# Causal mask of one-head score groups: from a TensorE matmul into VectorE's maximum

## What is computed

```
x = x + attention(layernorm(x))     # 32 query heads, 8 key/value heads, 64 wide, rotary, causal
x = x + ffn(layernorm(x))           # per-token int8 quantisation, one 256 x 256 product
scores = q @ k.T / 8;  scores = where(causal, scores, lowest float)
attn = softmax(scores);  out = attn @ v;  out @ Wo
```

## Time and profile before

| | |
|---|---|
| time, median of 3 runs | 802.25 us (799.59 to 802.53) |
| profiled execution, first to last instruction | 803.9 us |
| PE busy | 761.0 us (95%), 8230 matmuls |
| DVE busy | 629.2 us (78%), 1392 instructions |
| ACT busy | 628.4 us (78%), 1734 instructions |
| POOL busy | 569.1 us (71%) |
| mask matmuls (L720) | 352, of them 256 of one head |

### The profile page before, as it was taken

One profiled execution on the slowest core, in us unless ns is written; L12 is line 12 of the kernel. 1 busy time (PEld: TensorE's weight loads), 2 busy tenths in 40 slices (PEclk: granted clock), 3 DMA queues, 4 the chain that ended last, 5 costly groups with the idle time before them and its releaser, 6 DMA issues.

```text
span 803.9 us, 23412 instructions
## 1 busy us (share of the span) xinstructions
PE 761.0 (95%) x8230; PEld 640.0 (80%) x8230; DVE 629.2 (78%) x1392; ACT 628.4 (78%) x1734; POOL 569.1 (71%) x524
## 2 busy tenths in 40 slices
PE   5799999999999999999999999999999999999993
PEld 3578888888888887788888888888888888888782
DVE  5757787777787887777788888887788877877887
ACT  4577888787877887787788778887788778888873
POOL 3467868787768786877786887778686787686402
PEclk9899999999999999999999999999999999999996
DMA  8255544554555554455554455455454555454300
GB/s 267 56 119 114 130 119 118 132 141 111 127 121 108 118 118 93 117 117 119 115 121 108 113 128 120 104 128 122 106 117 107 122 116 126 93 116 97 87 8 27
DMA packets 56994, 90.99 MB, mean 113 GB/s; under 512 B 12592, under 2 KB 19248, under 8 KB 56880
## 3 DMA queue, kind: packets, MB, share of 16 engines
q1 hardware_dynamic: 53808, 79.02, 43.0%
q0 software_dynamic: 3072, 10.49, 5.0%
HBM read 16.06 MB, written 2.10 MB: 23 GB/s over the span
## 4 chain that ended last, share of the span: by engine, by line
PE 71%; DVE 6%; ACT 6%; SPq 5%; issue 5%; DMA 5%; POOL 2%; ACTq 0%; POOLq 0%; DVEq 0%
PE x_bank L621 21%; PE t_bank L733 14%; PE o_bank L749 11%; PE s_bank L717 9%; PE s_bank L718 8%; DMA qT<-wv 4%; PE s_bank L720 3%; PE t_bank L621 3%; PE ot_bank L800 2%; ACT prob L1028 2%; SPq L303 2%; DVE probT L1356 2%; SPq L337 1%; SPq L341 1%; DVE o_norm L1391 1%
## 5 line engine op out<-in xcount | busy, mean ns | idle before, releaser
L1028 ACT ACTIVATE prob<-s_bank,neg_max 128x384 f32<-128x384 f32 (+3 forms) x512 | 266.1, 530 | 64.9 <-DVE neg_max L1367 64.8
L1367 DVE TENSOR_REDUCE neg_max<-s_bank 128x1 f32<-128x384 f32 (+3 forms) x352 | 215.6, 635 | 60.3 <-PE s_bank L720 57.3
L1356 DVE SCALAR_TENSOR_TENSOR probT<-t_bank,probT 128x512 f16<-128x512 f32 x320 | 215.4, 681 | 29.6 <-ACT probT L1040 28.8
L1040 ACT ACTIVATE probT<-t_bank 128x512 f16<-128x512 f32 x320 | 189.0, 600 | 43.8 <-PE t_bank L733 38.8
L733 PE MATMUL t_bank<-ident,prob 128*128 128x128 f32 x1280 | 199.1, 278 | 5.1 <-DVE probT L1356 1.7
L717 PE MATMUL s_bank<-kT,qT 128*128 128x384 f32 (+3 forms) x512 | 178.3, 363 | 6.7 <-DMA qT<-wv 4.2
L491 POOL TENSOR_TENSOR wv<-raw,wv 128x512 fp32r<-128x512 f32 x62 | 79.4, 1280 | 134.2 <-ACT wv L989 134.2
L718 PE MATMUL s_bank<-kT,qT 128*128 128x384 f32 (+3 forms) x512 | 157.1, 322 | 0.0
L733 PEld LDWEIGHTS t_bank<-ident,prob 128*128 128x128 f32 x1280 | 137.6, 141 | 15.0 <-issue 7.5
L749 PE MATMUL o_bank<-value,probT 128*128 128x64 f16 x3840 | 138.5, 193 | 0.0
L749 PEld LDWEIGHTS o_bank<-value,probT 128*128 128x128 f16 x3840 | 131.4, 98 | 6.1
(11 more groups left out here) (123 smaller groups left out, 946.8 us busy)
## 6 DMA issues: line engine op xcount, KB each, us to landing
qT<-wv SPq DMA_DIRECT2D x248, 128.0 KB, 2.4
swp<-raw SPq DMA_DIRECT2D x320, 64.0 KB, 2.0
kT<-key_pair SPq DMA_DIRECT2D x128, 128.0 KB, 2.4
wg_raw<-in_w_group POOLq DMA_DIRECT2D x16, 384.0 KB, 4.9
wg_raw<-in_w_group POOLq DMA_DIRECT2D x16, 256.0 KB, 4.3
resid<-in_x SPq DMA_DIRECT2D x4, 512.0 KB, 7.5
out<-resid SPq DMA_DIRECT2D x16, 128.0 KB, 2.1
wo_stage<-in_w_out SPq DMA_DIRECT2D x4, 256.0 KB, 3.5
```

What stands on the lines that cost most here:

```text
L1028: nc.scalar.activation(prob[:, slot:slot + blocks, h, :], s_bank[G % SCORE_BANKS][:, at * n:(at + 1) * n].rearrange("p (k n) -> p k n", n= ...
L1040: nc.scalar.activation(turned_half[B % TURNED][HI], t_bank[B % TURN_BANKS][:, :], ACT.Copy, scale=PROB_SCALE).then_inc(probT_hi, 1)
L1356: nc.vector.scalar_tensor_tensor(out=turned_half[B % TURNED][LO], in0=t_bank[B % TURN_BANKS][:, :], scalar=PROB_SCALE, in1=turned_half[B % ...
L1367: nc.vector.tensor_reduce(neg_max[:, s % 2, u:u + len(heads)], s_bank[G % SCORE_BANKS][:, 0:len(heads) * n].rearrange("p (h n) -> p h n", ...
```

## The change

Groups with one head lose their mask matmul; their second score matmul signals instead. Their maximum becomes one tensor_tensor_reduce: it adds a row of 0 and -3e38 (mask_row, 512 columns in bf16, of which the last n are taken) to the bank, multiplies with -1, writes the result back into the bank and gives its minimum as neg_max. Their exponential reads the bank with scale -1. Groups 0, 9 and 10 stay as they are. To make room in SBUF the statistics get 8 slots instead of 16, in_inv shares the memory of root_t, and ones lies in an unused part of prob.

```
-        mask = sb("mask", [P, P], bf16)
+        mask_row = sb("mask_row", [P, SEQ], bf16)
...
-        stats = sb("stats", [P, TOK_TILES, 6], f32)
+        stats = sb("stats", [P, STATS, 6], f32)
...
-        in_inv = sb("in_inv", [P, TOK_TILES], f32)
+        in_inv = root_t
...
+        ones = prob[:, 3, 3, :].bitcast(bf16)[:, 0:P]
...
-            nc.gpsimd.memset(mask[:, :], 0.0).then_inc(const_zeroed, 1)
+            nc.gpsimd.memset(mask_row[:, :], 0.0).then_inc(const_zeroed, 1)
...
-                    nc.tensor.matmul(bank, q, kT[s % 2][:, LO, 0:n], start=False, stop=False, skip_group_check=True)
-                diagonals = s_bank[G % SCORE_BANKS][:, 0:len(heads) * n].rearrange("p (h n) -> p h n", n=n)[:, :, i * P:n]
-                nc.tensor.matmul(diagonals, ident_b[:, :], mask[:, :].unsqueeze(1).broadcast_to([P, len(heads), P]),
-                                 start=False, stop=True, skip_group_check=True).then_inc(scores_done, 1)
+                    last = nc.tensor.matmul(bank, q, kT[s % 2][:, LO, 0:n], start=False, stop=(len(heads) == 1),
+                                            skip_group_check=True)
+                if len(heads) > 1:
+
+                    diagonals = s_bank[G % SCORE_BANKS][:, 0:len(heads) * n].rearrange("p (h n) -> p h n", n=n)[:, :, i * P:n]
+                    last = nc.tensor.matmul(diagonals, ident_b[:, :],
+                                            mask_row[:, SEQ - P:SEQ].unsqueeze(1).broadcast_to([P, len(heads), P]),
+                                            start=False, stop=True, skip_group_check=True)
+                last.then_inc(scores_done, 1)
...
+                                     scale=-1.0 if len(SCORE_GROUPS[a][1]) == 1 else 1.0,
...
-                nc.vector.tensor_reduce(neg_max[:, s % 2, u:u + len(heads)],
-                                        s_bank[G % SCORE_BANKS][:, 0:len(heads) * n].rearrange("p (h n) -> p h n", n=n),
-                                        AX.X, ALU.max, negate=True).then_inc(max_done, 1)
+                if len(heads) > 1:
+                    nc.vector.tensor_reduce(neg_max[:, s % 2, u:u + len(heads)],
+                                            s_bank[G % SCORE_BANKS][:, 0:len(heads) * n].rearrange("p (h n) -> p h n", n=n),
+                                            AX.X, ALU.max, negate=True).then_inc(max_done, 1)
+                else:
+
+                    if G == 1:
+                        dve.wait_ge(const_ready, 6)
+                    bank = s_bank[G % SCORE_BANKS][:, 0:n]
+                    nc.vector.tensor_tensor_reduce(bank, bank, mask_row[:, SEQ - n:SEQ], -1.0, UNBOUNDED, ALU.add, ALU.min,
+                                                   neg_max[:, s % 2, u:u + 1]).then_inc(max_done, 1)
```

More of the change, by code:

```diff
@@ L27 @@
 MASKED = -3.0e38
+UNBOUNDED = 3.4e38
 PROB_SCALE = 2.0 ** 14
@@ L47 @@
 LN_STEPS = 5
+STATS = 2 * Q_TILES
 def attention_ffn_kernel(nc: bass.Bass, x: bass.AP, w_group: bass.AP, w_value: bass.AP, w_out: bass.AP,
@@ L76, in attention_ffn_kernel @@
         ident_b = sb("ident_b", [P, P], bf16)
-        mask = sb("mask", [P, P], bf16)
+        mask_row = sb("mask_row", [P, SEQ], bf16)
         zero = sb("zero", [P, 1], f32)
         magic = sb("magic", [P, 2], f32)
-        ones = sb("ones", [P, P], bf16)
         pow_rows = sb("pow_rows", [P, KV_HEADS], f32)
@@ L397, in _ @@
             load_group_weights(0)
-            nc.gpsimd.memset(ones[:, :], 1.0).then_inc(const_ready, 1)
+            nc.gpsimd.memset(ones, 1.0).then_inc(const_ready, 1)
             nc.gpsimd.memset(ident[:, :], 0.0).then_inc(const_zeroed, 1)
             nc.gpsimd.memset(ident_b[:, :], 0.0).then_inc(const_zeroed, 1)
-            nc.gpsimd.memset(mask[:, :], 0.0).then_inc(const_zeroed, 1)
+            nc.gpsimd.memset(mask_row[:, :], 0.0).then_inc(const_zeroed, 1)
             nc.gpsimd.memset(zero[:, :], 0.0).then_inc(const_zeroed, 1)
@@ L408, in _ @@
                                         pattern=[[-1, P]], channel_multiplier=1).then_inc(const_ready, 1)
-            nc.gpsimd.affine_select(out=mask[:, :], in_=mask[:, :], compare_op=ALU.is_ge, fill=MASKED, base=0,
+            nc.gpsimd.affine_select(out=mask_row[:, SEQ - P:SEQ], in_=mask_row[:, SEQ - P:SEQ], compare_op=ALU.is_ge, fill=MASKED, base=0,
                                     pattern=[[-1, P]], channel_multiplier=1).then_inc(const_ready, 1)
@@ L677, in _ @@
             for k in range(K_TILES):
-                last = nc.tensor.matmul(o_bank[:, :], ones[:, :], wv_abs[k], start=(k == 0), stop=(k == K_TILES - 1))
+                last = nc.tensor.matmul(o_bank[:, :], ones, wv_abs[k], start=(k == 0), stop=(k == K_TILES - 1))
             last.then_inc(wv_summed, 1)
@@ L1207, in done_statistics @@
                 dve.wait_ge(resid_added, part_no(s, f % Q_TILES) + 1)
-                nc.vector.bn_stats(stats[:, f, :], resid[:, t, :]).then_inc(stats_done, 1)
+                nc.vector.bn_stats(stats[:, f % STATS, :], resid[:, t, :]).then_inc(stats_done, 1)
             def tile_statistics(t):
-                nc.vector.bn_stats(stats[:, t, :], resid[:, t, :]).then_inc(stats_done, 1)
+                nc.vector.bn_stats(stats[:, t % STATS, :], resid[:, t, :]).then_inc(stats_done, 1)
             def aggregate(first_tile, end_tile, done):
@@ L1216, in aggregate @@
                     dve.wait_ge(stats_done, done + end_tile)
-                    nc.vector.bn_aggr(mean_var[:, t, :], stats[:, t, :]).then_inc(aggr_done, 1)
+                    nc.vector.bn_aggr(mean_var[:, t, :], stats[:, t % STATS, :]).then_inc(aggr_done, 1)
                 dve.wait_ge(aggr_done, done + end_tile)
```

## The result

The changed kernel takes 792.75 us (median of 4 runs, 791.54 to 793.81); the kernel before took 802.39 us beside it (4 runs, 799.59 to 803.44). The ratio is 0.9856 with a 95% interval of 0.983 to 0.9881, so 9.5 to 13.6 us are saved. The profiled execution took 792.76 us, with a span of 791.0 us.

A forecast was written before the change was run, and what follows sets the result against it. Up to turn 1, TensorE was taken to pace even steps and ScalarE's queue of exponentials odd ones. 16 x 0.45 + 16 x 0.15 = 9.6 us off the 802.25 us median gave 793 us, range 779 to 816.

The forecast's parts named there:

- The sum: Whole loop: 0.45 us saved in each of 16 even steps and 0.15 in each of 16 odd, 9.6 us.
- The mask's price: TensorE: a mask costs 0.07 us before transposes, 0.12 before score or projection matmuls; 25 us over the run.
- the rival that gives TensorE nearly everything: Whole loop: TensorE gets back nearly all 25 us of masks, 777 us (half way 785); chance 0.10.
- e: VectorE, each one-head maximum: time the accumulated minimum adds to the pass, taken as 0.09 us.
- rival on a dear e: VectorE's maxima: e from 0.125 to 0.165 us cancels the gain, chance 0.20; dearer makes it slower, chance 0.27.
- 5.5 e: Each step's path: e is paid about 5.5 times, for maxima 1 to 5 and 6 in part.
- The break-even at 0.145: VectorE's maxima: the forecast gain, 0.3 us a step on average, is used up at e of 0.145 us.
- the slower rivals: Maxima 1 to 5 set the pace from e of 0.165 us; 810 us at 0.19, 820 at 0.25; chance 0.27.
- The odd step: ScalarE's exponentials pace up to turn 1; TensorE keeps 0.15 us, from ScalarE's 0.1 and masks 7 and 8.
- The low half of block 0 starts when it did: VectorE, odd step, after maxima 1 to 5: closing gaps of 0.39 us offset 5 x 0.09 = 0.45 us.
- The queries' waits: TensorE, group 0: waits for the queries' DMA, 4.2 us over the run, move with the query path and stay.
- Even steps: TensorE keeps about 0.45 us; exponentials of groups 5 and 6 some 0.4 earlier, groups 7 and 8 about 0.25.

The follow-up runs named there:

- e11: The kernel before, unchanged, profiled a second time: 804.05 us in one run.
- e12: The changed kernel, unchanged, profiled a second time: 795.93 us in one run.
- e5: The changed kernel with a one-column ScalarE copy added in every step between block 0's copy and group 3's exponential: 794.41 us, ratio 0.988.
- e1: The changed kernel with the mask of one-head groups left out altogether, using the old tensor_reduce and old exponential: 791.17 us, ratio 0.9835.
- e3: The changed kernel with two one-element VectorE memsets ahead of each one-head maximum: 795.5 us, ratio 0.9887.
- e9: The changed kernel with the second pair of query placements put ahead of the half swap on SyncE: 794.15 us, ratio 0.9872.
- e10: The kernel before with the second pair of query placements put ahead of the half swap on SyncE: 801.76 us, ratio 0.9952.

## Why the prediction was right, point by point

**The sum.** 0.45 us in an even and 0.15 us in an odd step were predicted. Over all four kinds of step it is 0.51 and 0.43 in even, 0.21 and 0.11 in odd steps, 0.47 and 0.16 in the mean: 16 times both is 10.1 us, where the prediction had 9.6 (10.4 if the kinds are weighted by their steps, ten without and six with a quantised tile on either side). Steps 17 and 18 came at 21.83 and 22.13 us (predicted 21.9 and 22.2), PEld's waits for exponentials at 25.9, just above the 20 to 25 that were named. The ratio of the first comparison leaves room for a little more, 0.9881 at its end, where the predicted 793 on 802.25 is 0.9885; in the profiles the rest lies in the queries' gaps, 4.9 us less after, against which the loop starts 1.7 us later (group 0 of step 0 at 52.3 us in before's profile and 52.8 in e11's, at 54.0 in after's, 54.8 in e12's and 52.4 in e5's). Whether that start belongs to the change or to the execution stays open.

**The mask's price** held where it can be read. From the end of group 0's mask to the end of the out_product behind group 2, with no wait listed between, TensorE took 2.69 us in step 17 before (445.73 to 448.42) and 2.42 after (438.34 to 440.76): 0.27 us (0.25 to the start of the last of these matmuls) for two masks priced at 0.12 each. Its busy time fell by less, 0.57 and 0.53 us a step against 0.76 to 0.81 for eight; by busy time alone the price of the eight is not shown. That the full 25 us are out of reach is shown by e1: the rival that gives TensorE nearly everything fails for want of cover, not for VectorE's cost.

**e was mis-sized**: 0.09 us was predicted, 0 to 0.05 measured in VectorE's own time, 0.06 for an exponential that waits for the maximum. The reciprocal of the earlier trace rows, 0.08 us from start to start, was the wrong neighbour: it is recorded at 0.17 us and the read at 0.14, but the read takes less of the engine. The Trainium skill's page "VectorE: DVE Perf Modes", section "Two Vector instructions with no wait between them", is borne out in its rule, the accumulator's read is an instruction of its own in the trace. The 75 ns fixed per instruction of "Vector Engine (DVE) Microarchitecture Reference", section "Measured stream behaviour on trn2", are not seen on it: 0 to 50 ns are. The write of 512 columns into PSUM cost nothing beyond those 0 to 0.05 us, as taken. No rival on a dear e came about, and e3, with e near the 0.09 us assumed, still gains 9.1 us (1.13% of 803.97): the forecast held at its own e too.

**The slope of e** beyond 0.09 us stays unmeasured. The sum itself charges one e in an odd and two in an even step, and 5.5 e a step stands only beyond 0.09 us and in the sentence that reckons 2 or 3 us for 0.015. Had 5.5 e held all the way down, e at 0.02 would have made the kernel 12 us faster than predicted, 781 us, and e1, without any, 777; below 0.09 the steps move by far less, 0.05 to 0.09 us for the 0.07 of e3 and 0 to 0.14 us for all of the reduction's extra in e1. The argument named the reason itself, gaps ahead of the maxima, and they were larger than its 0.39 us, which it took between recorded ends: from start to start, ahead of add_product, one was 0.13 instead of 0.06 us (448.45 less 447.71, less 0.61). The break-even at 0.145, and so the point at which the slower rivals decide, rests on nothing measured.

**The odd step was right in size and half wrong in its reason.** The prediction let ScalarE's queue of exponentials set the pace up to turn 1, gave that stretch 0.1 us and the rest of the 0.15 to masks 7 and 8. e5 shows that the exponential of group 4 waits for its maximum, and the timelines show what the maximum waits for. TensorE, the end of group 4's scores in step 17, before and after:

```profile
449.71 0.23 PE L720 MATMUL s_bank<-mask,ident_b 128*128 128x128 bf16 x1
```

```profile
441.90 0.40 PE L720 MATMUL s_bank<-kT,qT 128*128 128x512 f32 x1
```

ScalarE, the exponential of group 4, before and after:

```profile
450.71 0.69 ACT L1028 ACTIVATE prob<-s_bank,neg_max 128x512 f32<-128x512 f32 x1
```

```profile
443.13 0.69 ACT L1035 ACTIVATE prob<-s_bank,neg_max 128x512 f32<-128x512 f32 x1
```

Both times maximum 4 starts 0.04 us behind the end of these scores (449.94 and 449.98, 442.30 and 442.34), in e1 it is even listed as waiting for them. And before the change too ScalarE had slack there: 0.78 us from the exponential of group 3 (449.93) to that of group 4, where two in a row take 0.67. So TensorE leads up to maximum 4, in the odd step too, and the masks ahead of it count: the maximum is 0.24 us earlier (5.56 to 5.32). By their price masks 1 to 4 would make it 0.38 (0.12, 0.12, 0.07 and group 4's own 0.07). Some of the rest goes where group 3's scores meet the exponentials of group 0: they started 0.26 us behind the last read of these before (448.26 and 448.00) and 0.05 behind it after (440.66 and 440.61). The exponential of group 4 is 0.18 us earlier (6.29 to 6.11), the other 0.06 being the accumulator's read, and turn 1, which waits for that exponential, moves by as much. "The low half of block 0 starts when it did" was wrong accordingly: 6.45 us after group 0, before 6.64. In sum the stretch up to turn 1 brings 0.18 us and not 0.1, and masks 7 and 8, which were to bring the rest, some 0.05.

**The queries' waits** were predicted to stay at 4.2 us. 0.9 us in the first profile looks like a miss, but they were 2.6 and 1.6 in the second pair, so their size belongs in part to the execution. Both pairs have less after the change, and with the swapped order the two kernels are closer together than with the old one, so the change may have a part in it; two pairs do not decide that. That SyncE's order makes these waits is shown by e9 and e10; why some executions have more of them stays open.

**Even steps** gained what was worked out, 0.43 to 0.51 us for 0.45, but some of the parts were too small. The exponentials of groups 5 and 7 in step 18, before and after:

```profile
476.36 0.58 ACT L1028 ACTIVATE prob<-s_bank,neg_max 128x384 f32<-128x384 f32 x1
...
478.44 0.58 ACT L1028 ACTIVATE prob<-s_bank,neg_max 128x384 f32<-128x384 f32 x1 [0.84 <-DVE neg_max L1367]
```

```profile
468.23 0.58 ACT L1035 ACTIVATE prob<-s_bank,neg_max 128x384 f32<-128x384 f32 x1
...
470.37 0.58 ACT L1035 ACTIVATE prob<-s_bank,neg_max 128x384 f32<-128x384 f32 x1 [0.91 <-DVE neg_max L1384]
```

Counted from group 0 (466.48 and 458.85), group 5 is 0.50 us earlier, where some 0.4 were predicted, and group 7 0.44 us, where it was 0.25. The timelines have turn 1 earlier by 0.50 us and turn 5 by 0.51: the whole gain is there at turn 1, and masks 7 and 8 add nothing to it. What takes up their 0.2 us was not taken apart by a run.

None of the versions tried beats the changed kernel but e1, 1.6 us below it with an interval that overlaps, which is a ceiling and no alternative.

## What to carry to other kernels

Work taken from the busiest engine comes back only as far as the next loop through the other engines lets it: leave the work out altogether once, and its time is the ceiling of every way to move it. Price an instruction by the distance from its start to the next one's, not by its recorded length, and apart from that by what it adds for the engine that waits for its result. Set a delay against the gaps that stand ahead of it before giving it the full slope. A view that lists no wait may hide a short one: compare the start with the end of what it needs. A wait whose length differs between two profiles of one kernel is no effect of a change until each has been profiled twice.

## What the hardware showed that was not expected

- The read of VectorE's accumulator is recorded at 0.14 us, yet the next instruction starts in the same moment as the read. The exponential that waits for the result comes 0.06 us later than behind tensor_reduce (0.79 against 0.73 us behind the maximum's start).
- A reduction of a float32 bank in PSUM with a bf16 row in SBUF that also writes 512 float32 columns back to PSUM goes from start to start in 0.61 us ahead of another such reduction and 0.65 us ahead of add_product, at or near the pace of the tensor_reduce (0.61) that writes one column.
- Two profiles of one kernel differ in the queries' gaps by 1.5 and 2.7 us (7.3 and 5.8, 2.4 and 5.1) while their undisturbed steps agree to 0.02 us.
